# A graph network's gate layer: one operand of three two-input VectorE instructions read from PSUM, and the seventh tile's product kept in another bank

## The reference, cut to what matters

```python
src, dst = (edge_index[0], edge_index[1])
edge_input = jnp.concatenate([x[src], edge_attr], axis=-1)
messages = _gelu(edge_input @ mW1 + mb1) @ mW2 + mb2
gates = jax.nn.sigmoid(_gelu(edge_input @ gW1 + gb1) @ gW2 + gb2)
aggregated = jax.ops.segment_sum(messages * gates, dst, num_segments=x.shape[0])
combined = jnp.concatenate([x, aggregated], axis=-1)
update = _gelu(combined @ uW1 + ub1) @ uW2 + ub2
h = x + update
```

## Time and profile before

| what | value |
|---|---|
| median of 3 runs | 3155.61 us (3154.09 to 3157.62) |
| profiled execution, time | 3152.14 us |
| profiled execution, span | 3150.0 us |
| gate layer's turns 3 to 95, first add to first add | 2277.45 to 3059.20 us |
| TensorE clock granted, mean | 0.938 |

### The profile page before, as it was taken

The page is one execution under the profiler, slowest core; times in us unless marked ns, Lnnn a source line. Parts: engine busy times, 40 slices in busy tenths (PEclk is TensorE's granted clock), DMA queues, the critical chain, the costliest instruction groups (busy, mean ns, idle before and its releaser), DMA issues.

```text
span 3150.0 us, 72359 instructions
## 1 busy us (share of the span) xinstructions
PE 2671.5 (85%) x25058; PEld 2203.0 (70%) x25059; DVE 2369.2 (75%) x6357; ACT 688.8 (22%) x1353; POOL 1183.8 (38%) x1205
## 2 busy tenths in 40 slices
PE   4677777889999997996999999997688888888884
PEld 1222222789999997995999999996576676666763
DVE  8888877762333347347899889997699999999986
ACT  0011222410000005011222222221233333233231
POOL 0000000000000000002777777772577777777771
PEclk9999988899999998997999999998799999999996
DMA  0000000000000000002544444441333333334330
GB/s 31 0 0 0 0 0 0 2 2 2 2 2 2 1 2 5 2 1 68 127 124 126 120 119 123 125 117 32 99 102 108 105 103 106 102 108 108 102 100 19
DMA packets 108155, 180.76 MB, mean 57 GB/s; under 512 B 36346, under 2 KB 69900, under 8 KB 107867
## 3 DMA queue, kind: packets, MB, share of 16 engines
q0 software_dynamic: 47824, 89.19, 11.5%
q1 hardware_dynamic: 60043, 87.59, 9.7%
HBM read 171.88 MB, written 4.80 MB: 56 GB/s over the span
## 4 chain that ended last, share of the span: by engine, by line
POOL 21%; DVE 17%; issue 9%; ACT 3%; DVEq 2%; PE 1%; DMA 1%; POOLq 0%; ACTq 0%
POOL gate_rows L1433 21%; DVE pre_space L1131 12%; ACT msg_rows L1085 1%; ACT msg_src_near L1061 1%; DVE msg_rows L1152 1%; DVEq L884 1%; DVE msg_rows L1160 1%; ACT msg_sums L1075 1%; DVEq L1177 0%; DMA first_rows<-pre_space 0%; DVE msg_aggT L1172 0%; PE msg_sums L1258 0%; DVE pre_space L1556 0%; PE gate_sums L1687 0%; DVE msg_rows L1158 0%
## 5 line engine op out<-in xcount | busy, mean ns | idle before, releaser
L1433 POOL DMA_INDIRECT gate_rows<-first_rows,all_src_i x637 | 648.4, 1018 | 198.9 <-issue 193.8
L1049 POOL DMA_INDIRECT msg_rows<-h_rows,all_src_i x539 | 513.5, 953 | 164.1 <-issue 158.0
L1036 POOL MEMSET pre_middle<- 125x1 f32 x1 | 0.1, 98 | 1467.2 <-POOLq L678 1467.2
L606 PE MATMUL hop_sums<-dense_work,dense_counts 125*128 125x192 f16 (+1 forms) x6250 | 532.1, 247 | 20.5 <-DVE dense_work L570 8.1
L1258 PE MATMUL msg_sums<-pre_parts,pre_space 125*128 125x192 f16 x6125 | 523.1, 246 | 29.8 <-DVE pre_space L1131 29.8
L606 PEld LDWEIGHTS hop_sums<-dense_work,dense_counts 125*128 125x128 f16 x6250 | 528.9, 98 | 23.6 <-DVE dense_work L570 9.9
L1258 PEld LDWEIGHTS msg_sums<-pre_parts,pre_space 125*128 125x128 f16 x6125 | 504.9, 98 | 36.6 <-DVE pre_space L1131 32.2
L1662 PE MATMUL gate_sums<-pre_space,pre_parts 125*96 125x384 f16 x2450 | 449.8, 344 | 5.6 <-DVE pre_parts L1530 5.6
L440 PE MATMUL cnt_sums<-cnt_hot,cnt_near 128*128 x1000 | 341.4, 410 | 107.4 <-DVE cnt_hot L372 106.2
L1131 DVE TENSOR_SCALAR pre_space<-msg_src_near,pre_node_no 125x640 f16<-125x640 f16 x1225 | 395.5, 396 | 17.0 <-ACT msg_src_near L1061 16.8
L1662 PEld LDWEIGHTS gate_sums<-pre_space,pre_parts 125*96 125x96 f16 x2450 | 309.9, 130 | 134.5 <-issue 29.6
(11 more groups left out here) (279 smaller groups left out, 3151.3 us busy)
## 6 DMA issues: line engine op xcount, KB each, us to landing
msg_edge<-edges SPq DMA_DIRECT2D x98, 384.0 KB
msg_src_row<-src_rows SPq DMA_DIRECT2D x49, 312.5 KB
gate_edge<-edges SPq DMA_DIRECT2D x98, 128.0 KB
gate_rows<-first_rows,all_src_i POOLq DMA_INDIRECT x637
gate_src_row<-on_src SPq DMA_DIRECT2D x49, 187.5 KB
msg_rows<-h_rows,all_src_i POOLq DMA_INDIRECT x539
gate_inputs<-on_edges SPq DMA_DIRECT2D x49, 48.0 KB, 2.0
first_rows<-pre_space SPq DMA_DIRECT2D x6, 375.0 KB
```

Of the source, the lines that this page charges most:

```text
L606: last = nc.tensor.matmul(sums[:, g0 + i, 0:wide], counts[0:NP, at:at + 128], half[frm][:, k, 0:wide], start=(k == 0), stop=(k == NT - 1))
L1049: nc.gpsimd.indirect_dma_start(out=rows[:, r, k, :], out_offset=None, in_=table, in_offset=bass.IndirectOffsetOnAxis(ap=src_i[:, at:at + 1 ...
L1433: nc.gpsimd.indirect_dma_start(out=rows[:, r, k, :], out_offset=None, in_=table, in_offset=bass.IndirectOffsetOnAxis(ap=src_i[:, at:at + 1 ...
```

## The change

Three operands move from SBUF into bank 3 of PSUM. `weigh_by` is a copy of `gw2`, made once; `aims` is a copy of half of the target numbers `dst_f`, made at the start and again at group 49; `gate_kept` is 1 + gate of one group, made by a new small VectorE instruction (128x8) in each turn, inside `link`. The one-hot's second instruction, so far a `scalar_tensor_tensor` that added the 1, becomes a plain `tensor_tensor`.

Bank 3 held the edge product of the fourth tile of an even group. `mix_edges` now makes 3 + 3 products for every group, and the seventh product of an even group goes to bank 7 beside the picked tile's (`seventh`), made in `mix_inputs`. VectorE adds it by a third instruction of 192 elements, after a wait for `on_mixed`. `added` therefore counts 3 for an even group and 2 for an odd one (`added_upto`). In even groups ScalarE now takes the gathered rows first and the picked tile after them; in odd groups the order stays. SP waits for `on_mixed` too before it loads a slot of `edge` again, and TensorE waits for `on_used` too before `sum_messages`.

```diff
+        seventh = sums[:, 7, ON[0] * 2 * D:(ON[0] + 1) * 2 * D]
+        aims = sums[:, 3, 0:ET // 2]
+        weigh_by = sums[:, 3, ET // 2:ET // 2 + D]
+        gate_kept = [sums[:, 3, 490 + GT * i:490 + GT * (i + 1)] for i in range(2)]
...
+        def added_upto(groups):
+
+            return 2 * groups + (groups + 1) // 2
...
                 sp.wait_ge(edge_mixed, group - SLOTS + 1)
+                sp.wait_ge(on_mixed, group - SLOTS + 1)
                 load_edges(group)
...
             def activate(group):
...
+                if group % 2:
+                    from_products()
+                    from_rows()
+                else:
+                    from_rows()
+                    from_products()
...
             link(nc.vector.tensor_scalar(gb2_sb[:, :], gb2_sb[:, :], 0.5, None, ALU.mult))
+            link(nc.vector.tensor_copy(weigh_by, gw2_sb[:, :]))
+            link(nc.vector.tensor_copy(aims, dst_f[:, 0:ET // 2]))
...
-                for half, k0, k1 in ((0, 0, n - 3), (1, n - 3, n)):
-                    to = rows[:, r, k0:k1, :]
-                    products = sums[:, 0:k1 - k0, 2 * D * half:2 * D * (half + 1)]
+                for half, k0 in ((0, 0), (1, n - 3)):
+                    to = rows[:, r, k0:k0 + 3, :]
+                    products = sums[:, 0:3, 2 * D * half:2 * D * (half + 1)]
                     nc.vector.tensor_tensor(to, to, products, ALU.add).then_inc(added, 1)
+                if n == 7:
+                    dve.wait_ge(on_mixed, group + 1)
+                    nc.vector.tensor_tensor(rows[:, r, 3, :], rows[:, r, 3, :], seventh, ALU.add).then_inc(added, 1)
...
-                nc.vector.tensor_tensor(values, values, gw2_sb[:, :].unsqueeze(1).to_broadcast([EP, GT, D]),
+                nc.vector.tensor_tensor(values, values, weigh_by.unsqueeze(1).to_broadcast([EP, GT, D]),
                                         ALU.mult).then_inc(weighed, 1)
...
                 slot = group % LAG
+                if group == NG // 2:
+                    link(nc.vector.tensor_copy(aims, dst_f[:, ET // 2:ET]))
                 dve.wait_ge(gate_out, group + 1)
+                link(nc.vector.tensor_scalar(gate_kept[group % 2], gate[:, group % 3, :], 1.0, None, ALU.add))
                 begin, end, base = group_steps(nc, g, mybir.EngineType.DVE, group)
...
-                    targets = dst_f[:, group * GT:(group + 1) * GT].unsqueeze(2).to_broadcast([EP, GT, SPAN])
-                    open_by = gate[:, group % 3, :].unsqueeze(2).to_broadcast([EP, GT, SPAN])
+                    targets = aims[:, group % (NG // 2) * GT:(group % (NG // 2) + 1) * GT].unsqueeze(2).to_broadcast([EP, GT, SPAN])
+                    open_by = gate_kept[group % 2].unsqueeze(2).to_broadcast([EP, GT, SPAN])
...
-                    nc.vector.scalar_tensor_tensor(out=hot, in0=open_by, scalar=1.0, in1=hot,
-                                                   op0=ALU.add, op1=ALU.mult).then_inc(onehot_ready, 1)
+                    nc.vector.tensor_tensor(hot, hot, open_by, ALU.mult).then_inc(onehot_ready, 1)
...
-                for half, n in enumerate((by_dma(group) - 3, 3)):
-                    for k in range(n):
+                for half in range(2):
+                    for k in range(3):
...
+                if by_dma(group) == 7:
+                    at = slice(DE * 3, DE * 4)
+                    nc.tensor.matmul(seventh, edge[at, group % SLOTS, 0, :], we[at, :], start=True, stop=True)
                 nc.tensor.matmul(to, ones[:, :], bias[:, 0:n, :], start=True, stop=False)
...
                 pe.wait_ge(rows_used, group + 1)
+                pe.wait_ge(on_used, group + 1)
```

More of the change, by code:

```diff
@@ L1465, in activate, with from_rows, from_products @@
                 r = rows[:, group % RING, 0:n, :]
-                act.wait_ge(on_mixed, group + 1)
+                def from_rows():
+                    act.wait_ge(added, added_upto(group + 1))
+                    nc.scalar.activation(gated[:, group % 2, 0:n, :], r[:, :, D:2 * D], ACT.Gelu).then_inc(gate_in, 1)
+                    nc.scalar.activation(passed[:, group % KEPT, 0:n, 0:D], r[:, :, 0:D], ACT.Gelu
+                                         ).then_inc(rows_used, 1)
+                def from_products():
+                    act.wait_ge(on_mixed, group + 1)
+                    nc.scalar.activation(gated[:, group % 2, n:GT, :], values[:, :, D:2 * D], ACT.Gelu
+                                         ).then_inc(gate_in, 1)
+                    nc.scalar.activation(passed[:, group % KEPT, n:GT, 0:D], values[:, :, 0:D], ACT.Gelu
+                                         ).then_inc(on_used, 1)
                 if group >= 2:
                     act.wait_ge(gate_sum, group - 1)
-                nc.scalar.activation(gated[:, group % 2, n:GT, :], values[:, :, D:2 * D], ACT.Gelu
-                                     ).then_inc(gate_in, 1)
                 if group >= KEPT:
                     act.wait_ge(group_done, group - KEPT + LAG + 1)
-                nc.scalar.activation(passed[:, group % KEPT, n:GT, 0:D], values[:, :, 0:D], ACT.Gelu
-                                     ).then_inc(on_used, 1)
-                act.wait_ge(added, 2 * (group + 1))
-                nc.scalar.activation(gated[:, group % 2, 0:n, :], r[:, :, D:2 * D], ACT.Gelu).then_inc(gate_in, 1)
-                nc.scalar.activation(passed[:, group % KEPT, 0:n, 0:D], r[:, :, 0:D], ACT.Gelu
-                                     ).then_inc(rows_used, 1)
+                if group % 2:
[4 more added lines that the diff above has]
+                    from_products()
             def open_gates(group):
@@ L1647, in mix_edges @@
                 if group:
-                    pe.wait_ge(added, 2 * group)
-                for half, n in enumerate((by_dma(group) - 3, 3)):
-                    for k in range(n):
+                    pe.wait_ge(added, added_upto(group))
+                for half in range(2):
+                    for k in range(3):
                         at = slice(DE * k, DE * (k + 1))
```

## The result

The kernel after takes 3242.45 us (median of 4 runs, 3241.14 to 3244.68), the kernel before 3155.53 beside it: a ratio of 1.0275, with a 95% interval of 1.0263 to 1.0287. It is 86.9 us slower; 97.4 was forecast. The two profiled executions, to the first of which the forecast adds its sum, lie 89.0 us apart.

A forecast was written before the change was run, and what follows sets the result against it. GpSimd and VectorE ran at nearly one pace, VectorE 1% faster; the change would make VectorE the bound. Terms summed to +97.4 us on the profiled 3152.14, 3249.5, plus 3.5 to the median: 3253 us, range 3232 to 3274.

The forecast's parts named there:

- The kept gate and its link: VectorE's register load waits for the new instruction behind the reduction: +1.07 us a turn in 98 turns, +104.9 us.
- Picks as before: VectorE's picks, held by gathers: little change expected; 0.15 us a turn either way, 15 us, only in the range.
- The seventh tile: VectorE's extra add in even groups: +3.2 us; its wait for `on_mixed` free, TensorE's product being 1 us ahead.
- PSUM as second input: VectorE's three instructions keep their length; L1556 loses 0.012 us of hold-up by gathers: -1 us.
- GpSimd's gathers: Gathers beside VectorE's instructions shorten by 68 ns, at most 43 us of GpSimd's time, worth nothing with VectorE the bound.
- The copy at group 49: VectorE's copy of 392 elements into PSUM: 0.57 us and 0.04 of link, +0.6 us.
- The ends and GpSimd's additions: Layer's end: gather waits go, -5.6 us; L1556's 6.7 us hold goes, 4.5 (0 to 6.7) put back for a pick.
- The register path: Rival: the small instruction fits VectorE's 0.33 us gap, turn stays 8.50, 3149 us; 5% together with the GpSimd rival.
- GpSimd's gain: Rival: VectorE's pace doesn't matter and GpSimd's 43 us give 3113 us; 5% together with the hidden register path.
- The rival that had half of the delay taken back by the picks: VectorE's picks held far less by gathers, so its turn shrinks: about no change to +50 us; 3%.
- TensorE's clock: Rival: TensorE falls to 1.2 of 2.4 GHz and becomes the bound, some 3,500 us in all; 3%.
- a sign that I had listed as one of being wrong: In the profile after: VectorE's adds waiting for TensorE's `on_mixed`, meaning the moved product is late.

The follow-up runs named there:

- small_alone: Kernel before plus one linked 128x8 instruction a turn, its result unused, all operands in SBUF: 3249.58 us, ratio 1.0298.
- seventh_alone: Kernel before with only the seventh product in bank 7, its third add and waits; no operand moved, no kept gate: 3154.07 us, ratio 1.0000.
- wait_at_use: Kernel after with the register load first and the kept gate waited for only ahead of the multiply that reads it: 3154.53 us, ratio 1.0001.
- adds_later: The `wait_at_use` kernel with GpSimd's two additions made to wait until the last picks are done: 3143.49 us, ratio 0.9964.
- load_first: Kernel after with the register load moved ahead of the small kept-gate instruction, the link staying: 3171.67 us, ratio 1.0049.

## Why the prediction was right, point by point

**What bounds it** (right). VectorE by its own turn, with GpSimd 1% behind. The kernel before with an early load, whose adds waited for gathers 51 times, shows how near the two were.

**The kept gate and its link, +1.07 us a turn** (right; 104.9 forecast). From the reduction's start to the accumulation's the mean rose from 1.302 to 2.356 us, by 1.054. The steps hold too: the small instruction starts 0.870 us behind the reduction (0.87 forecast) and took 0.159 (0.17). `small_alone` has the same 2.354 with nothing else of the change.

**Picks as before, within 0.15 us a turn** (the term that was mis-sized). The spacing fell from 0.2471 to 0.2366 us: 12.4 x 0.0105 = 0.130 us a turn, 12 us over 92 turns, where the sum had nothing. This is larger than the whole error of 10.5 us; the waits below take some of it back. I had allowed for it in the range and argued that a burst of gathers still covers the picks. With gathers left out both kernels come to the same floor, so it is the gathers that hold picks less.

A longer turn alone does not do it. `small_alone` has as long a turn, with all operands in SBUF: in turns 3 to 54, in which GpSimd never pauses, its spacing is 0.250 us, and in turns 60 to 92, in which it waits for a slot in each, 0.237. The kernel after has 0.239 in turns 3 to 31, before those waits, and 0.236 in turns 37 to 92, with them. A good part of it is single picks. In the kernel before 38 of them took over 0.4 us, all but one the third of a turn, each beside a gather that ended 0.44 to 0.46 us after the pick's start; the kernel after has 4, `small_alone` 43. So both GpSimd's pauses and the operands in PSUM go with closer picks. PSUM operands in a short turn leave a spacing of 0.238 to 0.245 us. What decides where in the turn a gather ends was not tested.

**The seventh tile, +3.2 us, its wait at nothing** (the wait was wrong). It cost 3.8 us: seven times TensorE's product was late, by up to 0.7 us. The cover of 1 us that I read from one turn does not exist in all of them. All seven adds start 2.9 to 3.1 us after the end of a stretch of 6.8 us in which TensorE was granted its lower clock (0.50, which is 1.2 of 2.4 GHz) and was busy nearly throughout. Four other such stretches have no wait behind them. One with a wait, and the add:

```profile
2509.40:2516.20 6.80, 6.77 (x29) 4.49 (x30) 5.29 (x15) 1.98 (x4) 5.28 (x6) 0.50 0.32 93
```

```profile
2519.07 0.35 DVE L1575 TENSOR_TENSOR gate_rows<-gate_rows,gate_sums 128x192 f32<-128x192 f32 x1 [0.60 <-PE gate_sums L1706]
```

Alone, the part costs nothing that can be measured.

**PSUM as second input, no change in length** (right). L1581 943 ns, L1612 688, L1614 687, against 956 in the earlier trace rows, and 692 and 693 for the one-hot pair before. The Trainium skill ("Perfetto Trace Analysis", Optimizing Scalar/DVE Operations) gives about 125 ns on PSUM against about 60 on SBUF, by which I had estimated 19 us more. No such step is seen here for a second operand in PSUM.

**GpSimd's gathers, no gain in the time** (right). They fell to 967 ns, and 93.2 us of waiting for `rows_used` took the gain. The wait came "in most groups", as forecast: in every group from 37 on, once the ring was full. In kernels whose GpSimd never paused the mean gather took 1014 ns with all operands in SBUF (`seventh_alone`) and 960 to 971 with all three in PSUM (`wait_at_use`, `adds_later`).
That a VectorE instruction with two SBUF inputs contends with a GpSimd instruction that reads SBUF is what the Trainium skill ("SBUF — State Buffer", Who interferes with whom) says; these means agree.

**The copy at group 49, +0.6** (right): 0.559 us for 392 elements, 0.57 forecast, and the next instruction started 0.59 us behind its start.

**The ends and GpSimd's additions, 4.5 us put back** (right). No add waited for a gather, and L1581 was not held. VectorE and GpSimd behind the last gathers of the kernel after:

```profile
3117.71 0.94 DVE L1581 TENSOR_TENSOR pre_space<-pre_space,gate_sums 128x768 f32<-128x768 f32 x1
...
3122.71 7.37 DVE L1546 TENSOR_SCALAR pre_space<-gate_src_near,pre_node_no 125x384 f16<-125x384 f16 x10
...
3117.42 5.28 POOL L1447 TENSOR_TENSOR pre_space<-all_h,pre_ub 125x2400 f32<-125x2400 f32 x1
3122.66 5.24 POOL L1449 TENSOR_TENSOR all_x<-all_x,pre_shift 125x2400 f32<-125x2400 f32 x1
```

L1581, with an input in PSUM, takes 0.94 us beside the first addition, where the earlier trace rows had 7.69. The picks behind it take 7.37 us for ten, 5.0 too many.

The size is luck. It was 5.0, 6.5, 8.2 and 10.8 us in four kernels with a pick held once, by how far the additions had got when the pick began (the 6.5 is that of `load_first`). My range of 0 to 6.7 was too narrow for the mechanism, though it held here.

**The sum again from the turn.** Less the hold, the turn is 9.469 us; it was 8.497, so it rose by 0.972. The parts: +1.054 (register path), +0.033 (one more add), +0.04 (its wait, 3.8 / 92), -0.013 (L1581), -0.01 (one-hots), -0.130 (picks) = 0.974. Over 92 turns 0.972 is 89.4 us, the hold adds 5.0 and the layer's end takes off 7.9: 86.5 from turn 3 to the last accumulation. The profiled executions are 89.0 apart and the medians 86.9.

**The rivals.** The register path did not stay hidden, and GpSimd's gain did not set the time. The rival that had half of the delay taken back by the picks named a real mechanism, but it took back 12% of the delay, 0.130 of 1.05 us. TensorE's clock was 0.91 in the layer and did not make it the bound; the only cost found is the wait of 3.8 us above, a sign that I had listed as one of being wrong.

## What to carry to other kernels

In this kernel a register load of 0.75 us and the loop's set-up ran beside a reduction of 0.95 us, and only 0.33 us of them showed. A small instruction with a wait for its own end, put between the two, made the whole path visible: it cost 1.05 us a turn, though it takes 0.16 itself. So issue loads ahead of such an instruction, and wait for a result where it is read.

Where two engines run at one pace, one edit at a time shows less than it is worth. Before an idea is dropped, look which engine waits next, and try it together with the edit that frees that one.

A long two-operand instruction on GpSimd should stand where VectorE has nothing to lose. Here taking away one victim handed the stall to the next.

## What the hardware showed unexpectedly

- GpSimd's two additions (5.27 and 5.24 us) mostly released a VectorE instruction only when both had ended: a pick was held for 10.8 us in one kernel and a two-SBUF-input multiply for 10.0 us in another:

```profile
3124.77 10.99 DVE L1557 TENSOR_TENSOR pre_space<-pre_space,pre_gw 128x768 f32<-128x768 f32 x1
...
3124.46 5.27 POOL L1439 TENSOR_TENSOR pre_space<-all_h,pre_ub 125x2400 f32<-125x2400 f32 x1
3129.68 5.25 POOL L1441 TENSOR_TENSOR all_x<-all_x,pre_shift 125x2400 f32<-125x2400 f32 x1
```

- That is not a rule. In both kernels without gathers the held instruction got through between the two additions, and the next one was held by the second. Here L1584 ends 0.55 us behind the first addition's end, the second addition takes 5.68 us instead of 5.2, and L1586 ends 0.55 us behind it. What makes the difference was not tested:

```profile
3000.71 4.88 DVE L1584 TENSOR_TENSOR gate_onehot<-pre_iota,pre_dst_f 128x512 f32<-128x512 f32 x1
3005.62 5.61 DVE L1586 SCALAR_TENSOR_TENSOR gate_onehot<-gate_gate,gate_onehot 128x512 f32<-128x512 f32 x1
...
2999.79 5.25 POOL L1438 TENSOR_TENSOR pre_space<-all_h,pre_ub 125x2400 f32<-125x2400 f32 x1 [704.17 <-ACT gate_passed L1477]
3005.00 5.68 POOL L1440 TENSOR_TENSOR all_x<-all_x,pre_shift 125x2400 f32<-125x2400 f32 x1
```

- The hold fell on picks, whose only tensor input is 384 f16 numbers a partition beside one number as scalar, as on instructions with two large inputs in SBUF; L1581 with an input in PSUM ran beside the same addition in 0.94 us.
- Gathers and picks hold each other up a little even with every two-input instruction reading PSUM: in the kernel after, a gather that starts beside a pick takes 1010 ns in the mean, and one that starts beside L1581, L1612 or L1614 takes 945.
